# A router's bias moved from TensorE to VectorE, its one-hot counts in bfloat16, and new places for the first phase's work

## The reference, cut to what matters

```python
xf = x.reshape(-1, d)                       # after a layernorm
cap = -(-n_tok // n_exp)                    # 512 places per expert
score = jax.nn.softmax(xf @ Wg + bg, axis=-1)
gate = jnp.max(score, axis=-1)
idx = jnp.argmax(score, axis=-1)
onehot = jax.nn.one_hot(idx, n_exp, dtype=jnp.int32)
pos = jnp.sum((jnp.cumsum(onehot, axis=0) - 1) * onehot, axis=-1)
keep = pos < cap
```

```python
align = jax.nn.softmax(jnp.tanh(scores), axis=2)
out = jnp.einsum('bst,tbd->sbd', align, x)
```

## Time and profile before

| | us |
|---|---|
| median of 3 runs | 3323.97 (3320.26 to 3329.62) |
| the profiled execution, its own time | 3321.13 |
| its span, first to last instruction | 3319.4 |
| PE busy | 3090.8 (93%) |
| DVE busy | 2329.1 (70%) |
| ACT busy | 1786.5 (54%) |
| POOL busy | 1284.2 (39%) |
| mean granted TensorE clock | 0.970 of full speed |

### The profile page before, as it was taken

The page is one execution under the profiler, slowest core; times in us unless marked ns, Lnnn a source line. Parts: engine busy times, 40 slices in busy tenths (PEclk is TensorE's granted clock), DMA queues, the critical chain, the costliest instruction groups (busy, mean ns, idle before and its releaser), DMA issues. The chain is left out here.

```text
span 3319.4 us, 57668 instructions
## 1 busy us (share of the span) xinstructions
PE 3090.8 (93%) x21302; PEld 2144.2 (65%) x21302; DVE 2329.1 (70%) x4781; ACT 1786.5 (54%) x3243; POOL 1284.2 (39%) x1933
## 2 busy tenths in 40 slices
PE   3799999999999998699999796899999999999997
PEld 2566666666666665366666454577777777777765
DVE  3588888888888887242111385687888778887784
ACT  3788888888888874211111132455555555555542
POOL 4366666666666653100000351133333333333332
PEclk8899999999999998799999898899999999999999
DMA  5887788887788872333324254433433334333320
GB/s 103 141 131 102 108 111 112 114 114 102 107 110 110 111 104 40 124 119 119 98 100 145 64 174 99 67 54 62 72 64 58 57 63 71 65 57 57 64 42 14
DMA packets 291101, 301.17 MB, mean 91 GB/s; under 512 B 35242, under 2 KB 278426, under 8 KB 290820
## 3 DMA queue, kind: packets, MB, share of 16 engines
q1 hardware_dynamic: 276420, 273.41, 48.7%
q0 software_dynamic: 6144, 15.68, 1.9%
q10 hardware_dynamic: 8256, 8.39, 0.8%
HBM read 95.51 MB, written 50.40 MB: 44 GB/s over the span
## 5 line engine op out<-in xcount | busy, mean ns | idle before, releaser
L493 DVE TENSOR_REDUCE xa_mx<-bank 128x2 f32<-128x512 f32 x1024 | 664.0, 687 | 257.0 <-PE bank L483 250.4
L597 ACT ACTIVATE xa_p<-bank 128x512 f32<-128x512 f32 x1024 | 566.5, 598 | 295.2 <-PE bank L587 270.6
L608 DVE SCALAR_TENSOR_TENSOR xa_p<-xa_p,bank 128x1024 f32<-128x1024 f32 x256 | 303.7, 1217 | 31.5 <-ACT xa_p L597 23.0
L620 PE MATMUL bank<-xa_p,xa_v 128*32 128x256 f32 x4096 | 278.6, 390 | 0.4 <-DVE xa_p L608 0.3
L1958 POOL DMA_INDIRECT sa_y<-expert_out,sa_s x64 | 68.6, 1072 | 526.6 <-POOLq L1853 484.5
L933 POOL TENSOR_SCALAR_AFFINE_SELECT xa_p<-xa_p 128x256 f32<-128x256 f32 x512 | 197.2, 407 | 175.4 <-ACT xa_p L924 175.2
L924 ACT ACTIVATE xa_p<-bank 128x384 f32<-128x384 f32 x512 | 231.0, 495 | 53.4 <-PE bank L912 42.0
L1747 ACT ACTIVATE ex_h<-bank,ex_b 128x512 f32<-128x512 f32 x64 | 44.0, 687 | 362.6 <-PE bank L1736 362.6
L1736 PE MATMUL bank<-ex_xt,ex_w 128*128 128x512 f32 x512 | 225.4, 599 | 0.7 <-ACT ex_xt L1727 0.7
L1766 PE MATMUL bank<-ex_w,ex_h 128*128 128x256 f32 x1024 | 224.0, 379 | 1.0 <-issue 0.9
L1766 PEld LDWEIGHTS bank<-ex_w,ex_h 128*128 128x128 f32 x1024 | 193.4, 190 | 28.1 <-issue 2.4
(11 more groups left out here) (284 smaller groups left out, 6925.8 us busy)
## 6 DMA issues: line engine op xcount, KB each, us to landing
ex_w<-ra_parts SPq DMA_DIRECT2D x384, 128.0 KB, 7.0
xa_ks<-xa_pk SPq DMA_DIRECT2D x384, 128.0 KB, 5.4
ex_w<-in_L_ffn_W SPq DMA_DIRECT2D x32, 1024.0 KB, 7.0
xa_qs<-xa_pq SPq DMA_DIRECT2D x192, 128.0 KB, 4.7
ex_w<-xa_pq SPq DMA_DIRECT2D x192, 128.0 KB, 4.5
ra_x<-in_x SPq DMA_DIRECT2D x32, 256.0 KB
xa_ctx<-in_ctx_t SPq DMA_DIRECT2D x64, 128.0 KB
queue<-zeros ACTq DMA_DIRECT2D x4, 2048.0 KB, 14.0
```

The costliest lines, as they stand in the source:

```text
L493: c.nc.vector.tensor_reduce(c.xa.row_max[:, :, n], halves(c.banks[2 + n % 2]), AX.X, ALU.max).then_inc(s.max_taken, 1)
L597: c.nc.scalar.activation(c.xa.p_beside[:, n // 2 % 4, :, n % 2, :], halves(c.banks[n % 2]), ACT.Exp, scale=SCALE).then_inc(s.exp, 1)
L608: c.nc.vector.scalar_tensor_tensor(out=p, in0=p, scalar=1.0, in1=c.banks[bank][:, :].unsqueeze(1).broadcast_to([P, TC, 2 * S]), op0=ALU.mi ...
L620: m = c.nc.tensor.matmul(bank[WIDE * quad:WIDE * quad + WIDE, at + q0:at + S], v[:, kc, 4 * g + quad, :], p(4 * g + quad, kc), start=(kc = ...
```

## The change

Router. The bias is loaded to all 128 partitions (and no longer waits for a clearing of rt_bg); the two bias matmuls per item go; DVE adds the bias as it takes the logits out of PSUM into a new tile rt_lg (L1166 in the changed kernel), and maximum and difference read that tile. The bank of the logits is free after this first operation, not after the second. The semaphore of the chain counts ten steps per item in place of nine. rt_hot, rt_before and the matrices causal and ones of the counts are bfloat16 (the counts that the matmul reads are whole numbers up to 64).

Places. Nearly all tables of the first phase have new numbers, and those of DVE and ACT in the third; the periods stay.

```diff
-    r.diff, r.eq, r.hot, r.ex, r.pos = (c.sb("rt_" + n, [P, TC, E]) for n in ("diff", "eq", "hot", "ex", "pos"))
+    r.logits, r.diff, r.eq, r.ex, r.pos = (c.sb("rt_" + n, [P, TC, E]) for n in ("lg", "diff", "eq", "ex", "pos"))
+    r.hot = c.sb("rt_hot", [P, TC, E], BF16)
...
-    r.before = c.ring("rt_before", 2, [P, TC, E])
+    r.before = c.ring("rt_before", 2, [P, TC, E], BF16)
...
-    c.step(c.dve_made, nc.vector.memset(r.bg[:, :, :], 0.0))
-    nc.sync.wait_ge(*c.all_of(c.dve_made))
     for k in range(TC):
-        load(c, r.bg[0:1, k, :], d["L0_ffn_bg"].partition_broadcast(1))
+        load(c, r.bg[:, k, :], d["L0_ffn_bg"].partition_broadcast(P))
...
+    nc.vector.wait_ge(c.loaded, 16 * c.loads)
...
     for tc in range(TC):
         out = c.banks[bank][:, tc * E:(tc + 1) * E]
-        c.nc.tensor.matmul(out, c.consts.ones[:, :], r.bg[:, tc, :], start=True, stop=False)
         for k in range(KC):
-            m = c.nc.tensor.matmul(out, r.xn_t[:, k, tc * P:(tc + 1) * P], r.wg[:, k, :], start=False, stop=(k == KC - 1))
+            m = c.nc.tensor.matmul(out, r.xn_t[:, k, tc * P:(tc + 1) * P], r.wg[:, k, :], start=(k == 0), stop=(k == KC - 1))
     m.then_inc(s.logits, 1)
-    c.bank_out[bank] = (s.chain, 9 * b + 2)
+    c.bank_out[bank] = (s.chain, 10 * b + 1)
...
     c.dve.wait_ge(s.logits, b + 1)
-    dve.tensor_reduce(r.mx[:, :], logits, AX.X, ALU.max).then_inc(s.chain, 1)
+    c.dve.wait_ge(s.chain, at)
+    dve.tensor_tensor(r.logits[:, :, :], logits, r.bg[:, :, :], ALU.add).then_inc(s.chain, 1)
     c.dve.wait_ge(s.chain, at + 1)
+    dve.tensor_reduce(r.mx[:, :], r.logits[:, :, :], AX.X, ALU.max).then_inc(s.chain, 1)
...
-    c.nc.tensor.matmul(out, c.consts.causal[:, :], r.hot[:, :, :].rearrange(flat), start=True, stop=False)
-    c.nc.tensor.matmul(out, c.consts.ones[:, :], r.before[b % 2][:, :, :].rearrange(flat), start=False,
+    c.nc.tensor.matmul(out, c.consts.causal_bf[:, :], r.hot[:, :, :].rearrange(flat), start=True, stop=False)
+    c.nc.tensor.matmul(out, c.consts.ones_bf[:, :], r.before[b % 2][:, :, :].rearrange(flat), start=False,
...
-        for b, _ in due(n, period, (735,)):
+        for b, _ in due(n, period, (739,)):
             pe_xa_turn(c, 6, b)
...
-        for b, _ in due(n, period, (276,)):
+        for b, _ in due(n, period, (244,)):
             dve_ra_normed(c, b)
```

More of the change, by code:

```diff
@@ L184, in setup_constants @@
     step(nc.gpsimd.tensor_copy(k.ident_bf[:, :], k.ident[:, :]))
-    step(nc.gpsimd.affine_select(out=k.causal[:, :], in_=k.ones[:, :], compare_op=ALU.is_ge, fill=0.0,
+    step(nc.gpsimd.memset(k.ones_bf[:, :], 1.0))
+    step(nc.gpsimd.affine_select(out=k.causal_bf[:, :], in_=k.ones_bf[:, :], compare_op=ALU.is_ge, fill=0.0,
                                  base=0, pattern=[[1, P]], channel_multiplier=-1))
@@ L1181, in act_rt_exp @@
     s, r = c.rt.s, c.rt
-    c.act.wait_ge(s.chain, 9 * b + 2)
+    c.act.wait_ge(s.chain, 10 * b + 3)
     c.nc.scalar.activation(r.ex[:, :, :], r.diff[:, :, :], ACT.Exp).then_inc(s.ex, 1)
@@ L1226, in pool_rt_place @@
     columns = slice(TC * b, TC * b + TC)
-    c.pool.wait_ge(s.chain, 9 * b + 9)
+    c.pool.wait_ge(s.chain, 10 * b + 10)
     c.pool.wait_ge(s.placed, at + 2)
@@ L1320, in pe_phase_a @@
             pe_xa_turn_sums(c, b, 1)
-        for b, _ in due(n, period, (934,)):
+        for b, _ in due(n, period, (935,)):
             pe_xa_turn_out(c, b)
-        for b, _ in due(n, period, (948,)):
+        for b, _ in due(n, period, (947,)):
             pe_a_project(c, 6, b)
@@ L1326, in pe_phase_a @@
             pe_rt_turn(c, 0, b)
-        for b, _ in due(n, period, (974,)):
+        for b, _ in due(n, period, (972,)):
             pe_rt_logits(c, 3, b)
@@ L1334, in dve_phase_a @@
     period = ROUND_A["dve"]
-    for n in range((B - 1) * period + 498):
-        for b, _ in due(n, period, (237,)):
+    for n in range((B - 1) * period + 499):
+        for b, _ in due(n, period, (236,)):
             dve_ra_stats(c, b)
-        for b, _ in due(n, period, (276,)):
+        for b, _ in due(n, period, (244,)):
             dve_ra_normed(c, b)
-        for b, _ in due(n, period, (293,)):
+        for b, _ in due(n, period, (294,)):
             dve_ra_index(c, b)
@@ L1365, in dve_phase_a @@
             dve_xa_normalise(c, b, 1)
-        for b, _ in due(n, period, (482,)):
+        for b, _ in due(n, period, (483,)):
             dve_a_end(c, 6, b)
@@ L1371, in dve_phase_a @@
             dve_rt_choose(c, 3, b)
-        for b, _ in due(n, period, (497,)):
+        for b, _ in due(n, period, (498,)):
             dve_rt_place(c, 3, b)
@@ L1377, in act_phase_a @@
     period = ROUND_A["act"]
-    for n in range((B - 1) * period + 620):
+    for n in range((B - 1) * period + 622):
         for b, _ in due(n, period, (353,)):
@@ L1414, in act_phase_a @@
             act_xa_raw(c, b, 0)
-        for b, _ in due(n, period, (580,)):
+        for b, _ in due(n, period, (579,)):
             act_xa_raw(c, b, 1)
@@ L1418, in act_phase_a @@
             act_xa_out_t(c, b)
-        for b, _ in due(n, period, (612,)):
+        for b, _ in due(n, period, (614,)):
             act_rt_xn_t(c, 0, b)
-        for b, _ in due(n, period, (619,)):
+        for b, _ in due(n, period, (621,)):
             act_rt_exp(c, b)
@@ L1426, in pool_phase_a @@
     period = ROUND_A["pool"]
-    for n in range((B - 1) * period + 346):
-        for b, _ in due(n, period, (183,)):
+    for n in range((B - 1) * period + 369):
+        for b, _ in due(n, period, (163,)):
             pool_ra_power(c, b)
@@ L2121, in dve_phase_d @@
     period = ROUND_D["dve"]
-    for n in range((STEPS_D - 1) * period + 40):
-        for b, _ in due(n, period, (16,), STEPS_D):
+    for n in range((STEPS_D - 1) * period + 41):
+        for b, _ in due(n, period, (17,), STEPS_D):
             dve_d_add(c, b)
@@ L2136, in act_phase_d @@
     period = ROUND_D["act"]
-    for n in range((STEPS_D - 1) * period + 28):
-        for b, k in due(n, period, (19, 20), STEPS_D):
+    for n in range((STEPS_D - 1) * period + 26):
+        for b, k in due(n, period, (20, 21), STEPS_D):
             act_d_xn_t(c, b, k)
@@ L2143, in act_phase_d @@
             act_d_tanh(c, b)
-        for b, _ in due(n, period, (27,), STEPS_D):
+        for b, _ in due(n, period, (25,), STEPS_D):
             act_d_exp(c, b)
```

145 lines of the change are left out of this document (73 added, 72 removed).

## The result

The changed kernel takes 3401.6 us (median of four, from 3396.4; one of the four, 3474, was disturbed and is left out of the ratio) against 3322.1 for the kernel before in the same session: 1.0237 times as long, 95% interval 1.022 to 1.0254. It is 79 us slower where 19 faster was forecast. The profiled execution took 3397.7 us, span 3395.5.

A forecast was written before the change was run, and what follows sets the result against it. PE was taken as nearly, not wholly, the bound, with VectorE full in half of each round. 14.4 + 2 + 1 + 1 + 1 = 19.4 us off 3321.1 gave 3301.7, as a median 3304; 8-in-10 range 3286 to 3325.

The forecast's parts named there:

- The sum itself: Whole kernel: 14.4 us from the rounds, 2 and 1 at the start, 1 at phase end, 1 in the third phase.
- the 0.69 us taken from PE: First-phase rounds: logits and counts together save PE 0.69 us per round, of which about 0.45 arrive.
- Logits: Router matmuls on PE: without the two bias matmuls, 0.88 us instead of 1.25, saving 0.37.
- the counts: Router's count matmuls on PE: 0.12 us in bfloat16 instead of 0.44 in float32, saving 0.32 (0.22 to 0.41).
- the sum for VectorE's fuller half: Second clip's end to last clip's: 14.6 us with ra_xn and the addition, 0.9 later; 0.4 after an earlier clip.
- the one on the choice: Router on VectorE: maximum and difference reading a tile cost nothing, between 0.1 us less and 0.1 more together.
- the two powers: POOL in the rounds: ra_rstd ready by 839.5 us at the latest; xa_rstd possibly 1.7 us later, about 2 in hand.
- (B): Rival for the rounds: VectorE takes the whole gain, round stays at 38.33 us or grows up to 0.23; 3322 us, chance 0.17.
- (A): Rival: PE bounds throughout, all 0.69 us and a tenth of pauses arrive per round; 3294 us, chance 0.20.
- (C): Rival, slower: POOL's power comes late for ra_xn between the clips, round 0.85 us longer; 3346 us, chance 0.13.
- its sign: What would show the late power: VectorE idle ahead of ra_xn, the idle ending with ra_rstd.
- xa_turn is no case of its own: PE in the rounds: xa_turn's new order waits about 1 us, but what stands behind it isn't needed before VectorE's indices.

The follow-up runs named there:

- e3: The changed kernel with POOL's two rt_before operations put back ahead of low_k instead of behind it: 3305.4 us, 0.9964 of the kernel before.
- e12: The changed kernel plus 36 extra 128-column bfloat16 matmuls per round, between logits and counts, into free bank 6: 3347.4 us, ratio 1.0092 to the kernel before.
- e2: The router of the kernel before, with the changed kernel's new places: 3400.6 us, ratio 1.0249 to the kernel before.
- e4: The changed kernel with the bias added in place in the bank, so maximum and difference read the bank: 3369.8 us, ratio 1.0155 to the kernel before.
- e14: e8 with the extra matmuls of e12: 3368.3 us, ratio 1.015 to the kernel before.
- e8: e4 with the one-hot made by two tensor_scalar operations of one tile and a column: 3405.9 us, ratio 1.0263 to the kernel before.
- e5: e2 with low_k put behind rt_before on POOL: 3414.3 us, ratio 1.0288 to the kernel before.
- e13: e5 with the extra matmuls of e12: 3385.9 us, ratio 1.0203 to the kernel before.
- e1: The changed router with all places of the kernel before: 3320.0 us, ratio 1.0006 to the kernel before.
- e11: The kernel before with the one-hot counts in bfloat16 alone: 3318.9 us, ratio 1.0005 to the kernel before.

## Why the prediction was wrong

**The sum itself** describes e3, the changed kernel but for one exchange on POOL. It forecast 14.4 us in the rounds and 5 outside them; e3's profile has 10.2 in the rounds (1172.0 to 1161.8 us from first to last logits) and 3.4 + 6.7 outside, 3.4 at the start and 6.7 behind the last logits. That its time is 3305.4, where I said 3304, is partly luck: the kernel before took 3316.7 in that session and not 3324, so e3 gains 11 us by the medians, not 19. The round is 38.13 and not 37.9: of the 0.69 us taken from PE 0.20 arrive, where I counted on 0.45. Nor are the 6.7 behind the last logits surely a gain: the kernels with the new places take between 1950.8 and 1958.4 us there, though these runs change nothing in the later phases, and the kernel before 1957.8. Logits went to 0.9 us, as forecast, and the counts to 0.1 or less, where I counted 0.12.

**The step that failed** is the sum for VectorE's fuller half, from the end of the second clip to that of the last: "Now it is 13.36 + 1.0 + 0.23 = 14.6: 0.9 later". That stretch takes 14.7 us in e3, but 16.2 in e12, where the one-hot is held, and 17.8 in the changed kernel, in the round shown above. The term left at nothing is the hold. The nearest sentence is the one on the choice: "Reading a tile in place of the bank for maximum and difference I cost at nothing, between 0.1 less and 0.1 more for the two". I bounded it by the operation's own records, 0.19 us; the difference took 1.65. What an operation of two SBUF tiles takes depends on what POOL runs beside it, and the change had moved just that. I followed POOL only to ask when its results are late (the two powers), never what its operations do to VectorE's while they run; low_k ahead of rt_before has no sentence in the prediction. Even with bank operands the places bring a hold (e2, e4), on rt_hot; the new operands only move it to an earlier step. Cost: 1.47 us per round by e12 against e3, 1.44 by e4's rounds at full clock.

The Trainium skill has a rule that speaks against this change, and the prediction didn't use it. "SBUF — State Buffer", section "Who interferes with whom", says that a VectorE instruction with two SBUF inputs contends with a GpSimd instruction that reads SBUF, and that the pair of ports the two engines share is an exclusive lock: whoever issues first has it for the whole instruction. The trace agrees on who is held and for how long: rt_diff ends within 0.06 us of low_k, with halves VectorE gets in between, and operations of bank and tile pass. It differs on the order: by the records rt_diff began 0.45 us before low_k, and still waited.

**The second failure** is in how I added. Every us of delay was one us. Here it was not: a pause of PE costs what it lasts and then a stretch at the lower clock. Mean rounds of the changed kernel in its steady part are 41.9 us: 38.13, and 1.47 for the hold, 0.6 for the late signal (e14 against e12) and 1.7 that is left, in rounds whose granted clock is 0.92 to 0.96. That this last term is clock is shown by the pairs that differ in added matmuls alone, 1.5 us from e8 to e14 and 1.6 from e5 to e13, and by e4's rounds, which differ by 1.2 to 2.4 us with the clock alone falling. Even e3's three rounds with such a stretch are 1.3 us longer than the others.

**The rivals.** (B) VectorE takes all of it, round 38.3: right for the old places (e1, e11), and I had it at 0.17. (A), PE the bound throughout, is refuted by e11 in the old places and by e3 in the new ones, where 0.20 of 0.69 us arrive. (C), POOL's power late for ra_xn: its sign, an idle VectorE ahead of ra_xn, is nowhere; but its place was near, since POOL's order is what decided. That xa_turn is no case of its own was right: PE's transposes begin 0.05 us behind xa_xn's end in e3 and 1.0 in the changed kernel, where xa_xn is 2.2 us later but PE as well.

**Not settled.** What makes TensorE's signal late beside a scatter, and why e2, e3, e4 and e12 escape. In the 20 us ahead of the second logits, the first whose signal is late in e8 (1.23 us behind the first matmul for e4's 1.10), PE's records of e4 and e8 agree to a few ns, and the transfers' shares nearly do, so these views don't show the cause. Nor is it settled how the low_k exchange acts on it: it removed the late signal with the changed router (e3) and brought it with the old one (e5 against e2). So e3 is a faster kernel here, by 0.36%, but not a sturdy one.

## What to carry to other kernels

When a table of places moves, list for every short VectorE operation with two SBUF inputs what GpSimd runs beside it, before and after; a 0.19 us step can take as long as the neighbour's operation. In a kernel whose TensorE is nearly full, price a new pause as the pause plus a stretch at half clock, or check by adding idle matmuls into a bank that is truly free: if the kernel gets faster with more work, the clock was the loss. And bring a new table's gain down to single exchanges, for each version of the work: here one of two neighbours was worth 96 us with the changed router and cost 14 with the old one.
